# An LSTM layer on four streams: the cell's tanh, its output product and the x products take other places in their queues

## The chip, the cores and the metric

The kernel runs on one core of one Trainium2 chip. The metric is the device time of one execution in microseconds (us), lower is better. Engines are named as the profile names them: PE is TensorE (PEld its weight loads), DVE is VectorE, ACT is ScalarE, POOL is GpSimd, SP issues DMAs.

## The reference, cut to what matters

Two layers run over x of shape (128 batches, 128 nodes, 128 features), each with a residual around it. The first is a spectral layer and needs an eigendecomposition. The second, which the change touches, is two graph convolutions and then LSTM sweeps over windows of 1, 2, 3 and 4 nodes, whose last hidden state replaces the window's last node:

```python
h = relu(einsum('ts,bsh->bth', adj, h @ Wg0 + bg0))
h = relu(einsum('ts,bsh->bth', adj, h @ Wg1 + bg1))
for p in range(1, 5):
    nw = 128 // p
    wins = h[:, :nw * p, :].reshape(B * nw, p, H)
    # over the p nodes of a window, from h = c = 0:
    #   i, f, g, o = split(x_t @ Wih[p-1].T + h @ Whh[p-1].T + bias[p-1])
    #   c = sigmoid(f) * c + sigmoid(i) * tanh(g);  h = sigmoid(o) * tanh(c)
    h = h.at[:, arange(nw) * p + p - 1, :].set(last hidden state)
x = x + h
```

## The kernel before

All data is fp32. The 128 batches are done in 8 rounds (`ROUNDS`) of 16; the 16 are 4 streams (`STREAMS`, numbered 0 to 3) of 4 batches (`GB`). The first third of the time is the eigendecomposition and layer norm, then the first layer; from about 525 us the second layer runs its 8 rounds.

A round of the second layer gives each stream a linear product (LIN), a second one (ZED), a graph convolution (CONV), 11 cells, a transpose back (TURN), and the mix for the next round (TURN+1). The 11 cells (`CELLS`) are, as window size p and step j: c0 and c1 (p=1, j=0, half of the nodes each), c2 and c3 (p=2), c4 to c6 (p=3), c7 to c10 (p=4). A cell works on 256 columns for c0 to c3, on 168 for c4 to c6 and on 128 for c7 to c10. A cell with j=0 has three gates and no recurrent part; one with j>0 has four gates, each the sum of an x product (weights times the window's nodes) and a recurrent product (weights times the hidden state of the step before).

`ORDER` is a list of pairs (step n, stream i) written out by a rule, and PE, ACT and DVE each walk the same list: streams 0 and 1 do step n, then streams 2 and 3 do step n-1, and so on. So two streams' short cells (j=0) stand between the other two streams' long ones. Each engine's queue is in order; engines meet by semaphores, one set per stream, that count up once a cell:

- PE, `cell`: waits, issues the x products of gates i and f (L939), waits for `hidden_ready`, issues their recurrent products (L944), then gates g and o (L949 the x products, L952 the recurrent ones), and signals `gates_ready`. Each fp32 product appears as two matmul instructions in the trace: 16 for a cell with j>0, 6 for one with j=0. A cell with j=0 waits for `hidden_ready` of the cell before at its first product. `turn_back` (L900) also waits for it.
- ACT, `gates` (L662, one activation a gate, out of the PSUM bank) and `cell_tanh` (L670, the tanh of the cell state c). For some cells an activation of the next round's input (L635) follows.
- DVE, `cell` (i*g, f*c, their sum: L1654, L1655, L1657; only L1651 where j=0) and `hidden` (o times tanh(c): L1666, or L1668 where it writes into the node array).

In the trace, BIG holds gates i and f, PV holds g and o, spare holds cell states, tanh values and hidden states. Below, F is the activation of gate f, I, G and O those of the others, T the tanh of a cell state, and H the output product in `hidden`.

Of the kernel before, what the change touches and what calls it, by code (L numbers as in the profile page):

```python
# [33 lines left out]
GATE_I, GATE_F, GATE_G, GATE_O = range(4)  # L34
# [6 lines left out]
CELLS = [(1, 0, 0, N // 2), (1, 0, N // 2, N // 2)] + [(p, j, 0, N // p) for p in range(2, SKIPS + 1) for j in range(p)]  # L41
# [18 lines left out]
def build(nc, t_in, out):  # L60
    with ExitStack() as ctx:
# [88 lines left out]
        gates_ready, acts_ready, cell_part, cell_ready = map(per_stream, ("gates", "acts", "cellp", "cell"))  # L150
        tanh_ready, hidden_ready, turned_ready, sum_ready = map(per_stream, ("tanh", "hidden", "turned", "sum"))
# [134 lines left out]
        def nodes(v):  # L286
            return v.rearrange("p (n b) -> p n b", b=GB)
# [208 lines left out]
        def _(act):  # L496
# [157 lines left out]
            def gates(it, c, i, qs):  # L654

                p, j, _, nw = CELLS[c]
                T = GB * nw
                for q in qs:
                    if q == GATE_F and j == 0:
                        continue  # L660
                    at = (p - 1) * 4 + q
                    last = nc.scalar.activation(gate_out[q][i][:, 0:T], gate(i, q, T),  # L662
                                                ACT.Tanh if q == GATE_G else ACT.Sigmoid, bias=bias[:, at:at + 1])
                if q == GATE_F:
                    last.then_inc(acts_ready[i], 1)

            def cell_tanh(it, c, i):
                T = GB * CELLS[c][3]
# [3 lines left out]
            def second_layer(it, more):  # L672
                act.wait_ge(tables, it + 1)

                nc.scalar.activation(act_scratch[:], ln[:, 2, 0:1], ACT.Sigmoid).then_inc(tables, 1)
                waiting = None
                for n, i in ORDER:
                    c = n - CELL
                    if n == LIN:
                        act.wait_ge(lin_kept[i], it + 1)  # L680
                        nc.scalar.activation(yS[i], linS[i], ACT.Relu).then_inc(y_ready[i], 1)
                    elif CELL <= n < TURN:
                        act.wait_ge(gates_ready[i], it * len(CELLS) + c + 1)
                        gates(it, c, i, (GATE_I, GATE_G, GATE_F))
                    if waiting:
                        cell_tanh(it, *waiting)
                        waiting = None
                    if CELL <= n < TURN:
                        gates(it, c, i, (GATE_O,))
                        waiting = (c, i)  # L690
                        if more and c in NORM_AT:
                            normalize(it + 1, i, NORM_AT.index(c), h1_ready)
# [13 lines left out]
        def _(pe):  # L706
# [179 lines left out]
            def mix(it, i, later):  # L886

                pe.wait_ge(h1_ready[i], it + 1)
                if later:
                    pe.wait_ge(acts_ready[i], it * len(CELLS))  # L890
                for b in range(GB):
                    last = nc.tensor.matmul(bank[i][0][:, b * N:(b + 1) * N], hs[i][:, b * D:(b + 1) * D], adjT[:],  # L892
                                            start=True, stop=True)
                last.then_inc(mix_ready[i], 1)
# [30 lines left out]
            def cell(it, c, i):  # L925

                p, j, w0, nw = CELLS[c]
                T = GB * nw
                todo = [q for q in (GATE_I, GATE_G, GATE_F, GATE_O) if j or q != GATE_F]
                xt = window(HS[i], p, j, w0, nw)  # L930
                if c == 0:
                    pe.wait_ge(H_ready[i], it + 1)
                elif j == 0:
                    pe.wait_ge(hidden_ready[i], it * len(CELLS) + c)
                else:
                    pe.wait_ge(tanh_ready[i], it * len(CELLS) + c)
                early = [q for q in todo if q in (GATE_I, GATE_F)]
                for q in early:
                    last = nc.tensor.matmul(gate(i, q, T), wT[:, 0, p - 1, q * D:(q + 1) * D], xt,  # L939
                                            start=True, stop=(j == 0))  # L940
                if j:
                    pe.wait_ge(hidden_ready[i], it * len(CELLS) + c)
                    for q in early:
                        last = nc.tensor.matmul(gate(i, q, T), wT[:, 1, p - 1, q * D:(q + 1) * D],  # L944
                                                hS[i][:, 0:T], start=False, stop=True)
                for q in todo:
                    if q in early:
                        continue
                    last = nc.tensor.matmul(gate(i, q, T), wT[:, 0, p - 1, q * D:(q + 1) * D], xt,  # L949
                                            start=True, stop=(j == 0))  # L950
                    if j:
                        last = nc.tensor.matmul(gate(i, q, T), wT[:, 1, p - 1, q * D:(q + 1) * D],  # L952
                                                hS[i][:, 0:T], start=False, stop=True)
                last.then_inc(gates_ready[i], 1)
# [24 lines left out]
        def _(dve):  # L979
# [364 lines left out]
            for f in range(2, F):  # L1344
                c = f % 2
# [300 lines left out]
            def cell(it, c, i):  # L1646
                p, j, _, nw = CELLS[c]
                T = GB * nw
                dve.wait_ge(acts_ready[i], it * len(CELLS) + c + 1)
                if j == 0:  # L1650
                    V.tensor_tensor(cS[i][:, 0:T], gI[i][:, 0:T], gG[i][:, 0:T], ALU.mult).then_inc(cell_ready[i], 1)  # L1651
                    return
                parts = it * PARTS + sum(2 for _, jj, _, _ in CELLS[:c] if jj)
                V.tensor_tensor(gI[i][:, 0:T], gI[i][:, 0:T], gG[i][:, 0:T], ALU.mult).then_inc(cell_part[i], 1)  # L1654
                V.tensor_tensor(gF[i][:, 0:T], gF[i][:, 0:T], cS[i][:, 0:T], ALU.mult).then_inc(cell_part[i], 1)  # L1655
                dve.wait_ge(cell_part[i], parts + 2)
                V.tensor_tensor(cS[i][:, 0:T], gI[i][:, 0:T], gF[i][:, 0:T], ALU.add).then_inc(cell_ready[i], 1)  # L1657

            def hidden(it, c, i):
                p, j, w0, nw = CELLS[c]  # L1660
                T = GB * nw

                dve.wait_ge(tanh_ready[i], it * len(CELLS) + c + 1)

                if j < p - 1:
                    V.tensor_tensor(hS[i][:, 0:T], gO[i][:, 0:T], tS[i][:, 0:T], ALU.mult).then_inc(hidden_ready[i], 1)  # L1666
                else:
                    V.tensor_tensor(window(HS[i], p, j, w0, nw), nodes(gO[i][:, 0:T]), nodes(tS[i][:, 0:T]),  # L1668
                                    ALU.mult).then_inc(hidden_ready[i], 1)
# [23 lines left out]
            def second_layer(it, more, extra=None):  # L1693

                waiting = None
                for n, i in ORDER:
                    if n == LIN:
                        dve.wait_ge(lin_ready[i], it + 1)
                        V.tensor_tensor(batches(linS[i]), batches(bank[i][2]),
                                        G0[:].unsqueeze(1).to_broadcast([N, GB, N]), ALU.add).then_inc(lin_kept[i], 1)  # L1700
                    elif n == ZED:
                        dve.wait_ge(z_ready[i], it + 1)
                        V.tensor_tensor(batches(zS[i]), batches(bank[i][3]),
                                        bg1B[:].unsqueeze(1).to_broadcast([N, GB, D]), ALU.add).then_inc(z_kept[i], 1)
                    elif n == CONV:
                        dve.wait_ge(conv_ready[i], it + 1)
                        V.tensor_scalar(nodes(HS[i]).rearrange("p n b -> p b n"), batches(bank[i][0]), 0.0, None,
                                        ALU.max).then_inc(H_ready[i], 1)
                    elif CELL <= n < TURN:
                        cell(it, n - CELL, i)  # L1710
                    elif n == TURN:
                        residual(it, i)
                    elif n > TURN and more:
                        keep_mix(it + 1, i)
                    if waiting:
                        hidden(it, *waiting)
                        waiting = None
                    if CELL <= n < TURN:
                        waiting = (n - CELL, i)
                    if extra:  # L1720
                        extra(n, i)
# [30 lines left out]
```

## Time and profile before

| | us |
|---|---|
| median of 3 runs (lowest, highest) | 1285.96 (1285.43, 1286.99) |
| the profiled execution: its own time | 1288.18 |
| span of its instructions | 1286.4 |
| busy: PE | 1206.5 (94%) |
| busy: PEld | 1074.1 (83%) |
| busy: DVE | 929.1 (72%) |
| busy: ACT | 903.5 (70%) |
| busy: POOL | 338.0 (26%) |

The profiled execution lies 2.2 us over the median. Its span is 1.8 us shorter than its own time. Matmuls are pipelined: a matmul's duration in the trace is longer than the distance to the next one, so PE's busy time covers short gaps between starts.

### The profile page before, as it was taken

The numbers are of one execution on the slowest core, as the hardware profiler recorded it, in microseconds if no ns is written. First come the engines' busy times: TensorE is split into PE (matmuls) and PEld (weight loads), VectorE is DVE, ScalarE is ACT, GpSimd is POOL, SyncE is SP. The second block draws the span as 40 slices with busy tenths as digits, with TensorE's granted clock in tenths as the row PEclk, the third lists the DMA queues.
The fourth block names the chain that finished last, engine by engine and source line by source line (L and its number), as shares of the span: only waits on it lengthen the run. The fifth ranks groups of instructions, "written<-read, shape, count | busy, mean of one in ns | idle before, by whom it ended". The sixth has DMA issues, their size and how long they took to land.

```text
span 1286.4 us, 26031 instructions
## 1 busy us (share of the span) xinstructions
PE 1206.5 (94%) x7973; PEld 1074.1 (83%) x7973; DVE 929.1 (72%) x4498; ACT 903.5 (70%) x3309; POOL 338.0 (26%) x1175
## 2 busy tenths in 40 slices
PE   9999999996645799999999999999999999999997
PEld 7788888875534688889889899899899899899897
DVE  8999999999999677667745645645645655656555
ACT  6788888868972122679578578578578578587676
POOL 0488888888888300001200000000000000000000
PEclk9999999988987799999999999999999999999999
DMA  9600000000000033000100100100000000000001
GB/s 264 148 2 2 2 2 2 2 1 1 2 1 1 16 97 86 2 1 2 33 0 0 33 0 0 33 0 9 24 0 16 16 0 16 16 0 17 17 1 34
DMA packets 43629, 28.83 MB, mean 22 GB/s; under 512 B 1521, under 2 KB 39441, under 8 KB 43537
## 3 DMA queue, kind: packets, MB, share of 16 engines
q1 hardware_dynamic: 43536, 27.81, 7.9%
q8 instruction: 33, 0.54, 0.2%
q14 instruction: 60, 0.48, 0.1%
HBM read 19.42 MB, written 8.39 MB: 22 GB/s over the span
## 4 chain that ended last, share of the span: by engine, by line
PE 60%; POOL 26%; DVE 6%; issue 5%; ACT 2%; ACTq 0%; DVEq 0%; POOLq 0%
PE bank L949 15%; PE bank L939 11%; PE bank L944 9%; PE bank L952 8%; POOL leaf L477 3%; PE bank L869 2%; PE bank L921 2%; PE bank L913 2%; PE bank L877 2%; PE bank L907 2%; PE bank L884 2%; PE bank L892 2%; POOL leaf L453 2%; POOL leaf L459 2%; ACT BIG L662 1%
## 5 line engine op out<-in xcount | busy, mean ns | idle before, releaser
L662 ACT ACTIVATE BIG<-bank,bias 128x128 f32<-128x128 f32 (+2 forms) x544 | 227.3, 418 | 160.8 <-PE bank L952 101.5
L949 PE MATMUL bank<-spare,wT 128*128 128x256 f32 (+2 forms) x1408 | 311.3, 321 | 0.0
L662 ACT ACTIVATE PV<-bank,bias 128x256 f32<-128x256 f32 (+2 forms) x704 | 302.6, 432 | 0.0
L949 PEld LDWEIGHTS bank<-spare,wT 128*128 128x128 f32 x1408 | 234.8, 191 | 13.2
L939 PE MATMUL bank<-spare,wT 128*128 128x128 f32 (+2 forms) x1088 | 226.4, 319 | 4.1 <-DVE spare L1668 2.7
L1654 DVE TENSOR_TENSOR BIG<-BIG,PV 128x128 f32<-128x128 f32 (+2 forms) x192 | 63.0, 328 | 207.3 <-ACT BIG L662 207.3
L939 PEld LDWEIGHTS bank<-spare,wT 128*128 128x128 f32 x1088 | 169.5, 191 | 19.3 <-DVE spare L1668 6.1
L952 PE MATMUL bank<-spare,wT 128*128 128x128 f32 (+2 forms) x768 | 169.7, 303 | 0.0
L944 PE MATMUL bank<-spare,wT 128*128 128x128 f32 (+2 forms) x768 | 141.7, 307 | 3.7 <-DVE spare L1666 1.2
L670 ACT ACTIVATE spare<-spare 128x256 f32<-128x256 f32 (+2 forms) x352 | 133.3, 379 | 4.2 <-DVE spare L1657 3.9
L952 PEld LDWEIGHTS bank<-spare,wT 128*128 128x128 f32 x768 | 125.2, 191 | 3.3
L944 PEld LDWEIGHTS bank<-spare,wT 128*128 128x128 f32 x768 | 113.8, 191 | 14.2 <-DVE spare L1666 10.8
L1651 DVE TENSOR_TENSOR spare<-BIG,PV 128x256 f32<-128x256 f32 (+2 forms) x160 | 60.8, 380 | 86.6 <-ACT PV L662 86.5
L736 PE MATMUL bank<-base 128*128 128x256 f32 x252 | 85.5, 421 | 0.0
L643 ACT ACTIVATE PV<-bank,b 128x512 f32<-128x512 f32 x32 | 22.0, 687 | 87.2 <-PE bank L869 87.2
L1657 DVE TENSOR_TENSOR spare<-BIG 128x128 f32<-128x128 f32 (+2 forms) x192 | 62.9, 327 | 6.6
L738 PEld LDWEIGHTS bank<-A,base 128*128 128x128 f32 x254 | 37.8, 187 | 34.7 <-DVE A L1100 34.4
L635 ACT ACTIVATE ahead<-X,ln 128x128 f32 (+1 forms) x128 | 62.9, 502 | 0.0
L1655 DVE TENSOR_TENSOR BIG<-BIG,spare 128x128 f32<-128x128 f32 (+2 forms) x192 | 61.6, 321 | 0.0
L1666 DVE TENSOR_TENSOR spare<-PV,spare 128x128 f32<-128x128 f32 (+2 forms) x192 | 61.6, 321 | 0.0
L809 PE MATMUL bank<-base,ahead 128*128 128x128 f32 x128 | 23.6, 313 | 38.7 <-ACT ahead L604 21.6
L1668 DVE TENSOR_TENSOR spare<-PV,spare 128x256 f32<-128x256 f32 (+2 forms) x160 | 59.6, 373 | 0.2 <-ACT spare L670 0.2
(495 smaller groups left out, 2773.2 us busy)
## 6 DMA issues: line engine op xcount, KB each, us to landing
spare<-in_x SPq DMA_DIRECT2D x32, 256.0 KB, 3.8
out<-X SPq DMA_DIRECT2D x32, 256.0 KB, 2.4
spare<-in_L_gnn_Wih SPq DMA_DIRECT2D x4, 256.0 KB, 4.9
spare<-in_L_gnn_Whh SPq DMA_DIRECT2D x4, 256.0 KB, 4.2
W<-in_L_gnn_W SPq DMA_DIRECT2D x2, 64.0 KB, 3.2
Wg<-in_L_gnn_Wg SPq DMA_DIRECT2D x2, 64.0 KB, 2.7
adj<-in_adj SPq DMA_DIRECT2D x1, 64.0 KB, 1.8
X<-in_x SPq DMA_DIRECT2D x4, 0.5 KB, 17.7
```

Of the source, the lines that this page charges most:

```text
L635: ins = nc.scalar.activation(hs[i][:, b * D:(b + 1) * D], X[:, at, :].rearrange("p b d -> p (b d)"), ACT.Relu, bias=ln[:, 3, at], scale=ln ...
L662: last = nc.scalar.activation(gate_out[q][i][:, 0:T], gate(i, q, T), ACT.Tanh if q == GATE_G else ACT.Sigmoid, bias=bias[:, at:at + 1])
L670: nc.scalar.activation(tS[i][:, 0:T], cS[i][:, 0:T], ACT.Tanh).then_inc(tanh_ready[i], 1)
L736: nc.tensor.matmul(banks[0][:, 0:2 * N], x_wide, base[:, 0:2 * N], start=True, stop=True).then_inc(xb_ready, 1)
L939: last = nc.tensor.matmul(gate(i, q, T), wT[:, 0, p - 1, q * D:(q + 1) * D], xt, start=True, stop=(j == 0))
L944: last = nc.tensor.matmul(gate(i, q, T), wT[:, 1, p - 1, q * D:(q + 1) * D], hS[i][:, 0:T], start=False, stop=True)
L949: last = nc.tensor.matmul(gate(i, q, T), wT[:, 0, p - 1, q * D:(q + 1) * D], xt, start=True, stop=(j == 0))
L952: last = nc.tensor.matmul(gate(i, q, T), wT[:, 1, p - 1, q * D:(q + 1) * D], hS[i][:, 0:T], start=False, stop=True)
L1654: V.tensor_tensor(gI[i][:, 0:T], gI[i][:, 0:T], gG[i][:, 0:T], ALU.mult).then_inc(cell_part[i], 1)
L1655: V.tensor_tensor(gF[i][:, 0:T], gF[i][:, 0:T], cS[i][:, 0:T], ALU.mult).then_inc(cell_part[i], 1)
L1657: V.tensor_tensor(cS[i][:, 0:T], gI[i][:, 0:T], gF[i][:, 0:T], ALU.add).then_inc(cell_ready[i], 1)
L1666: V.tensor_tensor(hS[i][:, 0:T], gO[i][:, 0:T], tS[i][:, 0:T], ALU.mult).then_inc(hidden_ready[i], 1)
```

## The change

On ACT the tanh of the cell before moves from behind gates i, g and f of a cell to behind gate i alone. On DVE the output product of the cell before moves from behind the products of a cell to ahead of them. On PE the x products of a cell with j>0 no longer wait for the tanh of the stream's cell before (`tanh_ready`) but for the read of its last gate, o; for that `acts_ready` now counts twice a cell.

```diff
@@ ACT, gates
-                if q == GATE_F:
-                    last.then_inc(acts_ready[i], 1)
+                    if q in (GATE_F if j else GATE_G, GATE_O):
+                        last.then_inc(acts_ready[i], 1)
@@ ACT, second_layer
-                        gates(it, c, i, (GATE_I, GATE_G, GATE_F))
+                        gates(it, c, i, (GATE_I,))
                     if waiting:
                         cell_tanh(it, *waiting)
                         waiting = None
                     if CELL <= n < TURN:
-                        gates(it, c, i, (GATE_O,))
+                        gates(it, c, i, (GATE_G, GATE_F, GATE_O))
@@ PE, mix and cell
-                    pe.wait_ge(acts_ready[i], it * len(CELLS))
+                    pe.wait_ge(acts_ready[i], it * (2 * len(CELLS)))
...
-                    pe.wait_ge(tanh_ready[i], it * len(CELLS) + c)
+                    pe.wait_ge(acts_ready[i], it * (2 * len(CELLS)) + 2 * c)
@@ DVE, cell and second_layer
-                dve.wait_ge(acts_ready[i], it * len(CELLS) + c + 1)
+                dve.wait_ge(acts_ready[i], it * (2 * len(CELLS)) + (2 * c + 1))
...
                 for n, i in ORDER:
+                    if waiting:
+                        hidden(it, *waiting)
+                        waiting = None
                     if n == LIN:
...
-                    if waiting:
-                        hidden(it, *waiting)
-                        waiting = None
```

ACT's queue at c8 of stream 0, in the loop over the rounds; BIG is gate i and, the second time, f, PV is g and o, spare is the tanh (here of c6 of stream 3). Before:

```order
L662 ACTIVATE BIG<-bank,bias 128x128
L662 ACTIVATE PV<-bank,bias 128x128
L662 ACTIVATE BIG<-bank,bias 128x128
L670 ACTIVATE spare<-spare 128x168
L662 ACTIVATE PV<-bank,bias 128x128
L635 ISA x2
L635 ACTIVATE ahead<-X,ln 128x128
```

The same place in the changed kernel:

```order
L662 ACTIVATE BIG<-bank,bias 128x128
L670 ACTIVATE spare<-spare 128x168
L662 ACTIVATE PV<-bank,bias 128x128
L662 ACTIVATE BIG<-bank,bias 128x128
L662 ACTIVATE PV<-bank,bias 128x128
L635 ISA x2
L635 ACTIVATE ahead<-X,ln 128x128
```

The tanh stands two activations earlier, and gates g and f one later; o and what follows keep their place.

DVE's queue at c9 of stream 3 (first three products), followed by the two TURN steps (L1677, the residual sum, of streams 0 and 1). Before:

```order
L1654 TENSOR_TENSOR BIG<-BIG,PV 128x128
L1655 TENSOR_TENSOR BIG<-BIG,spare 128x128
L1657 TENSOR_TENSOR spare<-BIG 128x128
L1666 TENSOR_TENSOR spare<-PV,spare 128x128
L1677 TENSOR_TENSOR X<-X,bank 128x512
L1666 TENSOR_TENSOR spare<-PV,spare 128x128
L1677 TENSOR_TENSOR X<-X,bank 128x512
```

In the changed kernel, with the output product of c9 of stream 2 now ahead of the three and that of stream 3 behind them:

```order
L1666 TENSOR_TENSOR spare<-PV,spare 128x128
L1654 TENSOR_TENSOR BIG<-BIG,PV 128x128
L1655 TENSOR_TENSOR BIG<-BIG,spare 128x128
L1657 TENSOR_TENSOR spare<-BIG 128x128
L1666 TENSOR_TENSOR spare<-PV,spare 128x128
L1677 TENSOR_TENSOR X<-X,bank 128x512 x2
```

Every output product moves one step of the list forward, past whatever DVE does there: a cell's products, a residual sum, or the ReLU behind CONV.

PE's queue at c5 of stream 0, with the semaphores waited for (the difference, - before, + changed):

```order
 L936 REGISTER_ALU
-L939 MATMUL bank<-spare,wT 128x168 [waits tanh0]
+L939 MATMUL bank<-spare,wT 128x168 [waits acts0]
 L939 MATMUL bank<-spare,wT 128x168
+L942 REGISTER_ALU
 L944 MATMUL bank<-spare,wT 128x168 [waits hidden0]
 L944 MATMUL bank<-spare,wT 128x168
```

No matmul moves; the first wait names another semaphore, and since the two waits now need different numbers, one register instruction stands between them.

## Rows read from the trace of the kernel before

**Rows 1.** Windows: busy us by engine in one round (x is the count)
```profile
697.50:791.95 94.45, 93.51 (x626) 86.23 (x625) 54.42 (x157) 70.08 (x223) 0.00 (x0) 1.00 0.04 11
```
**Rows 2.** Waits of PEld, 525 us to the end: total us, times, longest
```profile
PEld bank L944 <- DVE spare L1666: 10.8, 32, 0.4
PEld bank L939 <- DVE spare L1668: 6.1, 9, 0.7
PEld bank L939 <- ACT spare L670: 4.2, 16, 0.4
```
**Rows 3.** Timeline of PE at a round's front: start, us, instructions, [idle before]
```profile
716.64 3.60 PE L907 MATMUL bank<-BIG,Wg 128*128 128x512 f32 x8
720.07 1.95 PE L913 MATMUL bank<-Wg,PV 128*128 128x128 f32 x16
721.91 2.05 PE L921 MATMUL bank<-adjT,spare 128*128 128x128 f32 x16
723.80 1.95 PE L913 MATMUL bank<-Wg,PV 128*128 128x128 f32 x16
725.59 0.60 PE L939 MATMUL bank<-spare,wT 128*128 128x256 f32 x2
```
**Rows 4.** Timeline of PE, starts of two neighbouring cells, 256 and 168 columns
```profile
740.53 1.03 PE L939 MATMUL bank<-spare,wT 128*128 128x256 f32 x4
...
743.98 1.03 PE L939 MATMUL bank<-spare,wT 128*128 128x256 f32 x4
...
770.32 0.73 PE L939 MATMUL bank<-spare,wT 128*128 128x168 f32 x4
...
772.60 0.73 PE L939 MATMUL bank<-spare,wT 128*128 128x168 f32 x4
```
**Rows 5.** Timeline of PE, TURN to c10 of stream 2; one round later
```profile
706.68 1.16 PE L900 MATMUL bank<-base,spare 128*128 128x128 f32 x8
708.02 0.71 PE L939 MATMUL bank<-spare,wT 128*128 128x128 f32 x4 [0.18 <-ACT spare L670]
708.88 0.71 PE L944 MATMUL bank<-spare,wT 128*128 128x128 f32 x4
709.43 0.39 PE L949 MATMUL bank<-spare,wT 128*128 128x128 f32 x2
...
802.49 0.60 PE L939 MATMUL bank<-spare,wT 128*128 128x128 f32 x3 [0.18 <-ACT spare L670]
```
**Rows 6.** Timeline of PE, last x products of c2 of stream 3
```profile
749.16 1.03 PE L949 MATMUL bank<-spare,wT 128*128 128x256 f32 x4
```
**Rows 7.** Timeline of ACT and DVE, 256 columns, around c3 of stream 1
```profile
747.64 0.47 ACT L662 ACTIVATE BIG<-bank,bias 128x256 f32<-128x256 f32 x1 [1.58 <-PE bank L952]
...
748.37 0.48 ACT L662 ACTIVATE BIG<-bank,bias 128x256 f32<-128x256 f32 x1
748.72 0.42 ACT L670 ACTIVATE spare<-spare 128x256 f32<-128x256 f32 x1
749.03 0.48 ACT L662 ACTIVATE PV<-bank,bias 128x256 f32<-128x256 f32 x1
...
750.13 0.42 ACT L670 ACTIVATE spare<-spare 128x256 f32<-128x256 f32 x1
...
750.68 0.42 DVE L1668 TENSOR_TENSOR spare<-PV,spare 128x256 f32<-128x256 f32 x1
```
**Rows 8.** Timeline of ACT and DVE, 128 columns, c10 of stream 1
```profile
703.31 0.37 ACT L662 ACTIVATE BIG<-bank,bias 128x128 f32<-128x128 f32 x1 [0.45 <-PE bank L952]
...
703.83 0.37 ACT L662 ACTIVATE BIG<-bank,bias 128x128 f32<-128x128 f32 x1
704.08 0.32 ACT L670 ACTIVATE spare<-spare 128x128 f32<-128x128 f32 x1
704.28 0.38 ACT L662 ACTIVATE PV<-bank,bias 128x128 f32<-128x128 f32 x1
...
704.76 0.29 DVE L1657 TENSOR_TENSOR spare<-BIG 128x128 f32<-128x128 f32 x1
```

## The prediction

> **What bounds the kernel now.** I read the windows first, cut to one round of the second layer. PE is busy for 93.51 of 94.45 us, ACT for 70.08 and DVE for 54.42, at the full clock (1.00) [rows 1]. So PE sets the time there, and the change, which takes no matmul away, can gain only what PE loses to waits. How much that is, busy time does not tell, because matmuls overlap; the starts do. I take the distance between starts where nothing waits: 3.43/8 = 0.429 us for 512 columns and 1.79/16 = 0.112 for 128 [rows 3], 3.45/16 = 0.2156 for 256 and 2.28/16 = 0.1425 for 168 [rows 4]. From the code a round has 8 instructions of 512 columns (LIN), 136 of 256 (per stream 6 for each of c0 to c2, 16 for c3), 152 of 168 (6+16+16) and 328 of 128 (6+16+16+16 for the cells, 28 for ZED, CONV, mix and TURN). That makes 3.4 + 29.3 + 21.7 + 36.7 = 91.1 us. The round takes 802.49 - 708.02 = 94.47 [rows 5]. PE loses some 3.3 us a round.
>
> Then I asked for the waits of the weight loads, which name who is late: 32 waits for an output product before a recurrent product (4 a round), 16 for a tanh before x products (2 a round), 9 for an output product before a short cell (1 a round) [rows 2]. The change moves just these three. One further loss, 0.15 a round, it doesn't touch: CONV of stream 0 comes 0.05 late (721.91 - 720.07 = 1.84 for 1.79) and pays another 0.10 (723.80 - 721.91 = 1.89), the weight load that a stall leaves exposed [rows 3].
>
> The Trainium skill (Perfetto Trace Analysis, Identifying the Most-Contended Engine) says that matmul busy time doesn't tell the headroom and that the weight loads' does. By matmul idle time the gain would end at (94.45 - 93.51) x 8 = 7.5 us; by the starts at 3.3 x 8 = 26 [rows 1, 3 to 5]. The starts are what I go by.
>
> **The tanh, two activations earlier; F one tanh later.** In the 128-column cells F starts 0.52 and T 0.77 after I [rows 8]. In the new order T starts 0.26 after I, if its cell state is there. Its output product H then waits for nothing else: it ends at I + 0.26 + 0.32 (T) + 0.29 (a product's length, [rows 8]) + some 0.1 for the handoffs between engines (an estimate: F to T in [rows 7] is 1.76, three products in a row and F leave about 0.1 of it) = I + 1.0. Before, H stood behind the other stream's products, which end at 705.05, 1.74 after I [rows 8], and so ended at about I + 1.95. H comes some 0.95 us earlier: about half by each of the two moves, and neither alone brings it, since T behind the products of DVE, or H ahead of them with the late T, is still late.
>
> Is that enough? The waits come where two short cells stand between. Take c9 behind c8, with c7 of streams 2 and 3 between. PE's next start is 0.2 ahead of I (749.16 - 8 x 0.216 = 747.43 against 747.64 [rows 6, 7]). It has 12 x 0.112 = 1.34 of short cells and 0.45 of its own x products to do, and needs H's data a load (0.10) earlier: I - 0.2 + 1.79 - 0.1 = I + 1.5. H at I + 1.0 is in time by 0.5; before it was late by 0.45. With 168-column short or long cells the cover is longer and the answer the same, and c1 behind c0, late by about 0.2, has T 0.36 earlier ([rows 7], half of I to F). So I cost these at nothing left.
>
> Two places keep a wait.
> - **c4 behind c3** (no x products to cover it). New order from I at 747.64: T of stream 0's c3 at +0.37, G 0.31 later, F 0.36 later, at 748.68. F to the tanh of the same cell takes 750.13 - 748.37 = 1.76 (F, three products, handoffs); so T of stream 1 at 750.44, H from 750.89 to 751.31, and with handoff and load 751.46 [rows 7]. PE's slot for c4 of stream 0 is 749.16 + 4 x 0.216 = 750.02, now met, and for stream 1 it is 6 x 0.1425 later, 750.88. The stall moves one cell on, and is 0.58 us.
> - **c10 behind c9 of stream 2**, with only the TURN steps between. This place has both waits now: 2.75 us from 706.68 to 709.43 for 16 matmuls of 1.79, so 0.9 lost, 0.41 of it at the recurrent product (0.86 for four starts of 0.45) [rows 5]. The x products go free. For H, ACT must be on time: T waits for F + 1.22 + a handoff, F to T being 1.26 (between 1.22 and 1.30), while O and the next I fill only 0.5 of it [rows 8]. After the short cells, where ACT has more to do than PE, it is late, and the loop T, G (0.20 later), F (0.25 later), T again takes 0.20 + 0.25 + 1.26 = 1.71 against PE's 16 x 0.112 = 1.79, so it catches up by only 0.08 a cell. What stays lies between 0 (ACT on time) and 0.45 (as late as now); in a run of eight such items most of the lateness survives, and I take 0.35.
>
> **The x products** wait for O of a cell whose gates were read at least two items ago; they cover 0.45 us of H's way in the sum above. **The register instruction** on PE (L942, 6 a round): the like one, L936, stands ahead of the cell at 740.53, with no gap in the sequence in which I read the distance. I take 0, and 0.1 each, one exposed load [rows 3], as the other end: 4.8 us in all.
>
> **DVE's order.** H now goes ahead of CONV's ReLU, the residual sum and the mix copy, and these wait behind a tanh and a product, 0.42 each [rows 7]. PE has two cells c1 queued ahead of the first user of that ReLU, 12 x 0.216 = 2.6 us, and for the mix copy of stream 0 three more mixes of 8 x 0.112 and the two TURN steps. Hidden; without the cover it would be some 0.8 us a place.
>
> **The sum.** Per round 3.3 - 0.15 - 0.58 - 0.35 = 2.2 us, and 8 rounds 17.8. The last round has no L635 activations, so ACT is not late at c10 (0.35 more); its very last chain has T in front of G and F, 0.20 longer [rows 8], and nothing behind to hide it. Net 17.9 us. Against the profiled execution's 1288.18 that is 1270.3; that execution stands 2.2 over the median, and from 1285.96 I get **1268.1 us**.
>
> **The rivals.**
> - *ACT becomes the bound (slower).* If the loop T, G, F, T takes more than PE's 1.79 us, every 128-column cell with j>0 pays: 12 a round. It decides from where 12 x (loop - 1.79) is over 2.2, a loop of 1.97, 0.26 over my 1.71. At 2.1 us it would cost 3.7 a round and give 1285.96 + 8 x 1.5 = 1298. For it: T now waits at the head of ACT's queue with G, F and O behind it. Against: each link has its row [rows 8], and the 256-column loop has yet more room (0.31 + 0.36 + 1.76 = 2.4 against 3.45 [rows 4, 7]).
>  The Trainium skill (ScalarE: Activation LUTs, What ACT_TABLE_LOAD costs) lets activations that follow one another overlap by about 93 ns. By that, T to G would be 0.23 and G to F 0.29, an estimate that makes the loop 1.78, at PE's pace, and what stays at c10 the whole 0.45: 0.8 us less gain in all. The trace has 0.20 and 0.25.
> - *Half the gain.* ACT's lateness also reaches c9 and c6 behind the short cells, where my cover is 0.5 us: two more waits of 0.3 to 0.5 for streams 0 and 2. Gain 1.2 a round: 1276.
> - *No change.* Each stall only moves one cell on, as at c4. Against: the others have x products and short cells as cover. 1286.
> - *All but the fixed loss goes*: (3.3 - 0.15) x 8 = 25, 1261. It needs c4's chain to be 0.58 shorter; against: every link of it stands in a row.
>
> **How the numbers follow.** A measurement of this kernel tells about 0.2% (2.6 us) from no change. Chances: the forecast (1264 to 1272) 0.70, half the gain (to 1279) 0.14, nearly all lost waits gone (about 1261) 0.08, no change 0.03, slower 0.05. So faster 0.92, same 0.03, slower 0.05. The range that leaves out the last two and the farther halves of the second and third is 1262 to 1276; the register instructions' 4.8 us lie within it.
>
> **What the changed profile would show.** Rounds of 92.3 us. No waits of L939 for L670; L944's for L1666 down from 4 a round to 1, at c10 of stream 2, about 0.3; L939's for L1668 still 1 a round, now at c4 of stream 1. T 0.26 behind I where ACT is on time, and new short idle stretches of ACT ahead of L670, released by L1657. It would be wrong if ACT's loop exceeded 1.79 us, if the lateness of ACT reached c6 and c9, or if a gap stood ahead of every L944 (the register instruction).

## The result

| | before | changed |
|---|---|---|
| median (lowest to highest, 4 runs each) | 1286.37 (1285.43 to 1286.99) | 1266.48 (1265.86 to 1266.71) |
| ratio, 95% interval | | 0.9847 (0.9835 to 0.9859) |
| span of the profiled execution | 1286.4 | 1265.0 |
| a round of the second layer | 94.46 | 91.95 |

The change makes the kernel 19.9 us faster, and the interval of the ratio lies clear of 1. 17.9 were forecast, and 1266.48 lies in the range.

One round of the changed kernel in the windows view (columns as in [rows 1]):

```profile
690.30:782.25 91.95, 91.63 (x627) 85.87 (x626) 57.03 (x157) 70.68 (x223) 0.00 (x0) 1.00 0.04 12
```

The same matmuls in 2.5 us less. ACT and DVE run as many instructions as before (223 and 157). DVE shows 2.6 us more busy time for them: the durations of neighbours in its queue overlap less than they did, and each instruction is about as long as before. The waits of the weight loads over the second layer, to be compared with [rows 2], show which waits went:

```profile
PEld bank L939 <- DVE spare L1668: 4.8, 8, 0.8
PEld bank L913 <- ACT PV L681: 3.8, 7, 1.4
PEld bank L900 <- DVE spare L1668: 2.9, 4, 1.2
PEld bank L944 <- DVE spare L1666: 0.7, 1, 0.7
```

The 16 waits for a tanh (L670) are gone, and of the 32 for an output product ahead of a recurrent one (L944) a single one is left, in the first round. The wait of L939 for L1668 stays, once a round. The waits of L913 for ACT's ReLU (L681) at a round's front are loads that come early: in the middle rounds the matmuls of L913 lose no time by their starts, and only the one of 1.4 us, ahead of the second round, costs PE something (see e9). Those of L900 lie at the end of the first round and in the last one. The timeline of PE shows where the wait of L939 is now, at c4 of stream 1 (it was at stream 0):

```profile
743.38 0.45 PE L939 MATMUL bank<-spare,wT 128*128 128x168 f32 x2
743.66 0.73 PE L949 MATMUL bank<-spare,wT 128*128 128x168 f32 x4
744.72 0.55 PE L939 MATMUL bank<-spare,wT 128*128 128x168 f32 x2 [0.32 <-DVE spare L1668]
745.10 0.59 PE L949 MATMUL bank<-spare,wT 128*128 128x168 f32 x3
```

From 743.66 to 745.10 are 1.44 us for six starts of 0.1425, 0.86: the stall costs 0.58. ACT and DVE at the same place, to be compared with [rows 7]:

```profile
740.99 0.47 ACT L662 ACTIVATE BIG<-bank,bias 128x256 f32<-128x256 f32 x1 [1.58 <-PE bank L952]
741.36 0.41 ACT L670 ACTIVATE spare<-spare 128x256 f32<-128x256 f32 x1
741.67 0.47 ACT L662 ACTIVATE PV<-bank,bias 128x256 f32<-128x256 f32 x1
742.02 0.47 ACT L662 ACTIVATE BIG<-bank,bias 128x256 f32<-128x256 f32 x1
...
743.78 0.42 ACT L670 ACTIVATE spare<-spare 128x256 f32<-128x256 f32 x1 [0.56 <-DVE spare L1657]
...
744.23 0.43 DVE L1668 TENSOR_TENSOR spare<-PV,spare 128x256 f32<-128x256 f32 x1 [0.48 <-ACT spare L670]
```

The order is I, the tanh of stream 0, G, then F at 742.02, 1.03 behind I. From F to the tanh of the same cell it is 1.76; then H follows. The tanh now makes ACT wait 0.56 us, which costs nothing except through H.

### The profile page after: what moved, and what is told of

Read it like the earlier page. It is cut to its first block, busy times and chain, and to the rows that moved or that the text cites. A ratio compares the mean times of both kernels' runs of the same rounds, so it can differ in the third digit from the quotient of the medians.

```text
span 1265.0 us, 26139 instructions
## 1 busy us (share of the span) xinstructions
PE 1191.1 (94%) x7973; PEld 1070.5 (85%) x7973; DVE 949.4 (75%) x4498; ACT 908.5 (72%) x3309; POOL 335.2 (27%) x1175
## 4 chain that ended last, share of the span: by engine, by line
PE 48%; POOL 26%; issue 18%; DVE 4%; ACT 1%; POOLq 1%; DMA 1%; SPq 0%; DVEq 0%
PE bank L949 14%; PE bank L939 11%; PE bank L952 7%; PE bank L944 7%; POOL leaf L477 3%; PE bank L921 2%; POOL leaf L453 2%; PE bank L913 2%; POOL leaf L459 2%; PE bank L892 2%; PE bank L907 2%; POOL leaf L474 1%; POOL leaf L414 1%; POOL leaf L421 1%; PE bank L900 1%
## 5 line engine op out<-in xcount | busy, mean ns | idle before, releaser
L949 PE MATMUL bank<-spare,wT 128*128 128x256 f32 (+2 forms) x1408 | 311.3, 321 | 0.0
L662 ACT ACTIVATE PV<-bank,bias 128x256 f32<-128x256 f32 (+2 forms) x704 | 278.0, 425 | 0.0
L949 PEld LDWEIGHTS bank<-spare,wT 128*128 128x128 f32 x1408 | 234.8, 191 | 13.2
L939 PE MATMUL bank<-spare,wT 128*128 128x128 f32 (+2 forms) x1088 | 223.0, 315 | 2.7 <-DVE spare L1668 2.7
L939 PEld LDWEIGHTS bank<-spare,wT 128*128 128x128 f32 x1088 | 170.5, 191 | 12.6 <-DVE spare L1668 4.8
L952 PE MATMUL bank<-spare,wT 128*128 128x128 f32 (+2 forms) x768 | 169.7, 303 | 0.0
L670 ACT ACTIVATE spare<-spare 128x256 f32<-128x256 f32 (+2 forms) x352 | 129.3, 367 | 21.8 <-DVE spare L1657 17.3
L1668 DVE TENSOR_TENSOR spare<-PV,spare 128x256 f32<-128x256 f32 (+2 forms) x160 | 60.7, 380 | 107.5 <-ACT spare L670 107.5
L944 PE MATMUL bank<-spare,wT 128*128 128x128 f32 (+2 forms) x768 | 138.5, 303 | 0.5 <-DVE spare L1666 0.5
L944 PEld LDWEIGHTS bank<-spare,wT 128*128 128x128 f32 x768 | 114.4, 191 | 4.0 <-DVE spare L1666 0.7
L1657 DVE TENSOR_TENSOR spare<-BIG 128x128 f32<-128x128 f32 (+2 forms) x192 | 63.0, 328 | 6.6
```

What stands on the lines that cost most here:

```text
L670: nc.scalar.activation(tS[i][:, 0:T], cS[i][:, 0:T], ACT.Tanh).then_inc(tanh_ready[i], 1)
```

## The experiments

"Round" is the distance between the starts of LIN on PE (L907 or its line in that kernel) in two neighbouring rounds near the middle of the second layer. From the third round to the seventh it repeats within 0.01 us in a trace, except for one round of `e5_wide_tanh`, which is 1.5 us longer than its neighbours (see there). So it tells more than the time does. The rows it is taken from, one pair shown, of the changed kernel:

```profile
894.07 0.59 PE L907 MATMUL bank<-BIG,Wg 128*128 128x512 f32 x1
...
986.02 0.59 PE L907 MATMUL bank<-BIG,Wg 128*128 128x512 f32 x1
```

| kernel | round | median | ratio to before (95%) |
|---|---|---|---|
| before | 94.46 | see below | 1 |
| changed | 91.95 | 1266.48 | 0.9847 (0.9835, 0.9859) |
| e1_tanh | 96.50 | 1305.32 | 1.0137 (1.012, 1.0153) |
| e2_out | 93.40 | 1278.98 | 0.993 (0.9913, 0.9946) |
| e3_x | 94.46 | 1288.04 | 1.0003 (0.9994, 1.0013) |
| e4_tanh_out | 92.14 | 1270.26 | 0.9866 (0.9849, 0.9882) |
| e5_wide_tanh | 95.03 | 1294.2 | 1.0064 (1.0049, 1.008) |
| e6_early_ig | 91.61 | 1262.68 | 0.9817 (0.9803, 0.983) |
| e7_early_var | 91.94 | 1266.87 | 0.9848 (0.9833, 0.9863) |
| e8_both | 91.60 | 1262.2 | 0.9814 (0.98, 0.9827) |
| e9_short_inverse | 91.94 | 1264.56, one run | |
| e10_tanh_behind_g | 92.21 | 1268.18, one run | |

Each ratio is to runs of the kernel before on the same chip in the same series. Its median was 1286.37 beside the changed kernel, 1287.63 beside e1 to e4 and 1286.68 beside e5 to e8, so the ratios compare better than the medians. For e9 and e10 there is one run each, beside one of the kernel before (1285.7), and their rounds carry the argument.

### One part alone

**e1_tanh**, only ACT's order (the signal for the gates read still counts once a cell):

```diff
-                if q == GATE_F:
-                    last.then_inc(acts_ready[i], 1)
+                    if q == (GATE_F if j else GATE_G):
+                        last.then_inc(acts_ready[i], 1)
...
-                        gates(it, c, i, (GATE_I, GATE_G, GATE_F))
+                        gates(it, c, i, (GATE_I,))
...
-                        gates(it, c, i, (GATE_O,))
+                        gates(it, c, i, (GATE_G, GATE_F, GATE_O))
```

> The kernel before with the tanh moved behind the first gate on ACT, and nothing else. Theory A (the gain comes from the two moves together; the output product H is what PE waits for): H still stands behind the next cell's products on DVE, and these now start one tanh later (0.20 to 0.31 us), so H and the next tanh come later at every place where short cells stand between. Slower: a round of 96.4 us instead of 94.46, 1285.96 + 8 x 1.9 = 1301. Theory B (each move brings its share alone): about half of the gain, a round of 93.2, 1276. Theory C (the x products' wait is the cause): the tanh is released earlier, so the 2 waits a round for it go, a round of 93.6, 1279.

Measured: the round grows by 2.04 us. Its waits over one round, from the waits view:

```profile
PEld bank L944 <- DVE spare L1666: 2.6, 4, 0.9
PEld bank L939 <- DVE spare L1668: 2.2, 5, 1.0
```

No wait for a tanh is left. The waits for H grew: those of L944 are 2.6 us against 1.4 in a round before. L939 waits for its H five times where it waited once; among these are c4, now for two streams, c1 and c7. DVE and ACT at a 128-column cell show why:

```profile
889.11 0.37 ACT L662 ACTIVATE BIG<-bank,bias 128x128 f32<-128x128 f32 x1
889.37 0.30 ACT L670 ACTIVATE spare<-spare 128x128 f32<-128x128 f32 x1
...
890.22 0.29 DVE L1654 TENSOR_TENSOR BIG<-BIG,PV 128x128 f32<-128x128 f32 x1 [0.92 <-ACT BIG L662]
...
890.95 0.29 DVE L1666 TENSOR_TENSOR spare<-PV,spare 128x128 f32<-128x128 f32 x1
```

The tanh starts 0.26 behind I, but H ends at 891.24, 2.13 behind I, where the prediction read 1.95 in the kernel before. This is theory A: the tanh is early, but H stands behind products that start later. B and C fall.

**e2_out**, only DVE's order:

```diff
                 for n, i in ORDER:
+                    if waiting:
+                        hidden(it, *waiting)
+                        waiting = None
...
-                    if waiting:
-                        hidden(it, *waiting)
-                        waiting = None
```

> The kernel before with the output product ahead of the next cell's products on DVE, and nothing else. Theory A: H then waits for the late tanh only, which comes 0.77 us behind the first gate; H is some 0.5 us earlier where it was late by 0.45, the waits for the tanh ahead of x products stay. A round of 93.3, 1286 - 9 = 1277. Theory B (additive, half each): 93.2, 1276. Theory C (the x wait): unchanged, 94.5, 1286.

Measured: 1.06 us a round less. Over one round:

```profile
PEld bank L939 <- DVE spare L1668: 0.9, 1, 0.9
PEld bank L939 <- ACT spare L670: 0.6, 2, 0.4
```

The four waits of L944 are gone, those for the tanh stay. By the round's length A and B can't be told apart here (93.3 and 93.2); e1 excludes B.

**e3_x**, only the counter, which counts twice a cell as in the change, and PE's wait:

```diff
...
-                    pe.wait_ge(tanh_ready[i], it * len(CELLS) + c)
+                    pe.wait_ge(acts_ready[i], it * (2 * len(CELLS)) + 2 * c)
```

> The kernel before with the x products waiting for the last gate's read instead of the tanh (with the counter that counts twice), and nothing else. Theory A: the x products start earlier, but the recurrent products behind them wait for the same H as before, so PE loses the same time a few matmuls later. No change: a round of 94.3 to 94.5, 1286. Theory C: the 2 waits a round for the tanh go, 0.7 to 0.9 us a round, 1279.

Measured: no change. The timeline of PE at c10 of stream 2, to be compared with [rows 5]:

```profile
705.21 1.15 PE L900 MATMUL bank<-base,spare 128*128 128x128 f32 x8
706.20 0.61 PE L939 MATMUL bank<-spare,wT 128*128 128x128 f32 x4
707.40 0.71 PE L944 MATMUL bank<-spare,wT 128*128 128x128 f32 x4 [0.59 <-DVE spare L1666]
707.95 0.39 PE L949 MATMUL bank<-spare,wT 128*128 128x128 f32 x2
```

From L900 to L949 it is 2.74 us, as in [rows 5] (2.75). The x products start with no wait, and the recurrent ones wait longer. C falls: the two waits for a tanh in [rows 2] cost nothing of their own.

**e4_tanh_out**, both moves, PE waiting for the tanh as before; shown against the changed kernel, and the counter counts once a cell again:

```diff
...
-                    pe.wait_ge(acts_ready[i], it * (2 * len(CELLS)) + 2 * c)
+                    pe.wait_ge(tanh_ready[i], it * len(CELLS) + c)
```

> The changed kernel with the x products waiting for the tanh again, as before: both moves, no new wait on PE. Theory A: nearly the whole gain, a round of 92.0 against 91.95 for the full change, up to 0.2 more at c10 of stream 2, where only the transposes stand between; 1267 to 1268. Theory C: most of the gain is lost, a round of 92.8 or more, 1274.

Measured: 92.14, 0.19 a round over the full change. The x wait is worth 8 x 0.19 = 1.5 us once the tanh and H are early, and nothing alone. H's move together with the x wait, without the tanh's move, was not run, so what the tanh's move adds to those two is not known apart.

### The position, and ACT's loop

**e10_tanh_behind_g**:

```diff
-                        gates(it, c, i, (GATE_I,))
+                        gates(it, c, i, (GATE_I, GATE_G))
...
-                        gates(it, c, i, (GATE_G, GATE_F, GATE_O))
+                        gates(it, c, i, (GATE_F, GATE_O))
```

> The changed kernel with the tanh behind gates i and g instead of behind i alone. Theory A (what counts is when H is there, and there is a margin at most places): H comes one activation later (0.25 to 0.36 us) where ACT is on time, F comes no earlier or later. Only c1 of stream 0 (0.16) and c10 of stream 2 (0.16) lose their margin: a round of 92.2 against 91.94, 1268 to 1268.5. Theory J (being at the first place is what gives the gain): the round goes back towards 93.4, the value with the tanh at its old place, 1273 or more.

Measured: 92.21. The first place is worth 0.27 us a round over the second; J falls.

**e5_wide_tanh** lengthens the suspected loop:

```diff
                 act.wait_ge(cell_ready[i], it * len(CELLS) + c + 1)
+                T = 384 if T == 128 else T
                 nc.scalar.activation(tS[i][:, 0:T], cS[i][:, 0:T], ACT.Tanh).then_inc(tanh_ready[i], 1)
```

> The changed kernel, in which the tanh of the 128-column cells runs over 384 columns (the extra 256 are not used, so the outputs stay the reference's): ACT's loop tanh, G, F, tanh grows from 1.71 to 1.92 us, above PE's 1.79 a cell. Theory A (the rival priced in the prediction: ACT becomes the bound from 1.79 on, at 12 cells a round): 12 x 0.13 = 1.6 us a round more, less what was in time by a margin, so 93.3 to 93.5 a round and 1266.5 + 11 to 13 = 1278 to 1280; the new waits of PE stand at c9, c10 and the transposes. Theory D (the loop has slack elsewhere, since ACT is busy for only three quarters of the time): under 0.4 us a round, 1267 to 1270.

Measured: 95.03, so 3.1 us a round more, where A said 1.4 to 1.6 and D under 0.4. ACT's timeline in this kernel:

```profile
886.63 0.52 ACT L671 ACTIVATE spare<-spare 128x384 f32<-128x384 f32 x1
887.06 0.35 ACT L662 ACTIVATE PV<-bank,bias 128x128 f32<-128x128 f32 x1
887.31 0.36 ACT L662 ACTIVATE BIG<-bank,bias 128x128 f32<-128x128 f32 x1
...
888.56 0.52 ACT L671 ACTIVATE spare<-spare 128x384 f32<-128x384 f32 x1
```

The tanhs stand 1.93 apart, against PE's 1.79, and PE waits at the transposes, here those of another round:

```profile
800.38 0.64 PE L901 MATMUL bank<-base,spare 128*128 128x128 f32 x4
802.12 0.75 PE L901 MATMUL bank<-base,spare 128*128 128x128 f32 x4 [1.10 <-DVE spare L1669]
```

So the mechanism of the slower rival exists: a loop of 1.71 costs nothing in the middle rounds, one of 1.93 does. Its price of 12 x (loop - 1.79) is too low by half. PE doesn't lose the time cell by cell. By the starts of a middle round, 1.4 of the 3.1 us stand at the transposes, where the wait is 1.10, 1.0 at c10 of stream 2 right behind them, and the rest at the 128-column cells around and at the next round's front; nothing is lost at c7. ACT's lateness adds up over the cells and PE pays it where nothing covers. What the price leaves out is, I think, the four short cells c7: there PE needs 6 x 0.112 = 0.67 and ACT is the longer one anyway, so 0.21 more for each tanh counts in full (0.8), and H itself ends 0.21 later at each of the two places that wait. 1.7 + 0.8 + 0.4 = 2.9. That is argued, not shown apart.

The one round that is 1.5 us longer has its cause in the windows view, where the column behind POOL's is the granted clock as a share of the full one:

```profile
1089.30:1092.80 3.50, 3.50 (x18) 3.50 (x19) 2.27 (x6) 1.85 (x6) 0.00 (x0) 0.53 0.01 4
```

Here the granted clock is 0.53, the lower level (1.2 GHz) but for the edges; in the rest of the round it is 1.00 (2.4 GHz). The 128-column matmuls in this stretch start 0.213 apart instead of 0.112, which makes the 1.5 us. PE had stood idle for 1.09 and 0.73 us in the 3.2 us before. The other middle rounds of this kernel have the same two stalls and keep the clock; the first round also has such a stretch. So the stalls alone don't decide it. No run shows what does. The changed kernel shows no such stretch in the second layer before its last round's end.

### What is still left

**e6_early_ig**:

```diff
+                    elif j and q == GATE_G:
+                        last.then_inc(relu_ready[i], 1)
...
-                dve.wait_ge(acts_ready[i], it * (2 * len(CELLS)) + (2 * c + 1))
...
+                dve.wait_ge(relu_ready[i], ROUNDS + it * (PARTS // 2) + sum(1 for _, jj, _, _ in CELLS[:c] if jj) + 1)
                 V.tensor_tensor(gI[i][:, 0:T], gI[i][:, 0:T], gG[i][:, 0:T], ALU.mult).then_inc(cell_part[i], 1)
+                dve.wait_ge(acts_ready[i], it * (2 * len(CELLS)) + (2 * c + 1))
```

> The changed kernel, in which DVE's product i times g waits for gate g alone, not for f, in cells with j>0. Theory A (the wait left at c4 of stream 1 is the chain F, three products, tanh, H): F to tanh is shorter by one product's start distance, 0.34 us at 256 columns, so the wait there falls from 0.58 to 0.24. A round of 91.6, 1264 (0.2% below the changed kernel). Theory E (the wait at c4 is set elsewhere, by ACT's order or DVE's queue): no change, 91.95, 1266.5.

Measured: 91.61, 0.34 less. DVE and ACT at c3 of stream 1 in this kernel, where i times g is L1657 and the tanh L672:

```profile
740.16 0.47 ACT L662 ACTIVATE BIG<-bank,bias 128x256 f32<-128x256 f32 x1
...
740.30 0.43 DVE L1657 TENSOR_TENSOR BIG<-BIG,PV 128x256 f32<-128x256 f32 x1
740.67 0.42 DVE L1659 TENSOR_TENSOR BIG<-BIG,spare 128x256 f32<-128x256 f32 x1
...
741.59 0.42 ACT L672 ACTIVATE spare<-spare 128x256 f32<-128x256 f32 x1 [0.22 <-DVE spare L1661]
```

i times g now runs beside F, and F to the tanh is 741.59 - 740.16 = 1.43 instead of 1.76. E falls; the wait left at c4 is this chain. The time fell by more than the 2.7 us expected, to 1262.68: the middle rounds bring 0.34 each, but the first brings 1.13 (92.53 us against 93.66) and the last with what follows it 0.8. In the first round the wait at c10 of stream 2 (the row at 609.09 below) is gone in this kernel, so that wait too hangs on the chain from F to the tanh.

The first two rounds of the changed kernel take 93.66 and 92.85, not 91.95. Three kernels ask why.

**e7_early_var** and **e8_both** (this edit and the last):

```diff
-                elif (n, i) == (CELL + 8, 3):
+                elif (n, i) == (CELL + 7, 3):
```

> The changed kernel, in which the six variance instructions of the first round stand four items of the list earlier, so that POOL's power of 10.58 us starts about 4.9 us earlier. Theory F (the first two rounds gained less, 2.2 and 1.9 us against 2.5, because POOL's power ends late and holds DVE's inverse, the mix copies and so the front of the second round): the front of the second round loses 0.7 us less and the first round's c10 wait of 0.68 goes; rounds 1 and 2 together 1.2 to 1.7 us shorter, 1265. Theory G (it is the batch statistics on DVE alone, not POOL): no change, 1266.5.

> The changed kernel with both of the last two edits (i times g early, variance early). If A and F hold, they add: 0.34 x 8 + 1.5 = 4.2 us, 1262.3.

Measured for e7: POOL's power of 10.58 us now runs from 597.62 instead of 603.98 and so ends at 608.20, the first round shrinks by 0.36 to 93.30, and the second stays at 92.85. Of PE's three idle stretches there in the changed kernel,

```profile
609.09 0.71 PE L944 MATMUL bank<-spare,wT 128*128 128x128 f32 x4 [0.51 <-DVE spare L1666]
616.74 0.74 PE L900 MATMUL bank<-base,spare 128*128 128x128 f32 x4 [0.21 <-DVE spare L1668]
621.59 0.38 PE L913 MATMUL bank<-Wg,PV 128*128 128x128 f32 x1 [0.55 <-ACT PV L681]
```

the first stays in e7,

```profile
609.57 0.71 PE L944 MATMUL bank<-spare,wT 128*128 128x128 f32 x4 [0.51 <-DVE spare L1666]
```

and so does that of L913, by its starts as long as before (0.71). Only that of the transposes (L900) is gone. Theory F is right for 0.36 us and wrong for the rest: it expected the c10 wait and the front to shrink too. Its median, 1266.87, can't be told from the changed kernel's.

e8 reaches 1262.2 where 1262.3 was expected, and part of that is luck. By the rounds the early product i times g brings 4.0 us instead of 2.7, and the early variance 0.8 on top of it instead of 1.5: the first round is 91.81, 0.72 less than in e6. The medians of e6 and e8 are within each other's intervals.

**e9_short_inverse**:

```diff
-                    inverse(slice(FIRST, BATCH))
+                    V.reciprocal(ln[:, 3, FIRST:BATCH], ln[:, 2, FIRST:BATCH]).then_inc(ln_done, 1)
```

> The changed kernel, in which the inverse of the first round is one instruction of DVE instead of six, so that the norm scales of the last 64 batches are wrong: it leaves out about 1.2 us of DVE's work at the end of the first round. The variance moved earlier left the 0.71 us wait at the second round's front as it was, so POOL is not its cause. Theory H (DVE comes to the mix copies and to the sums behind LIN late because of the six instructions): the wait of ZED's products for ACT at the second round's front falls from 0.71 to 0.15 or less, the second round from 92.85 to 92.1, and the transposes' wait of 0.38 at the end of the first goes. Theory I (it is something else in the unrolled first round, as the longer walk of code): the second round stays at 92.85.

This kernel leaves out five of the six instructions, so its outputs are not the reference's. Measured: the second round takes 92.02, the first 93.14. PE at the second round's front:

```profile
616.61 3.17 PE L907 MATMUL bank<-BIG,Wg 128*128 128x512 f32 x7
619.61 2.03 PE L913 MATMUL bank<-Wg,PV 128*128 128x128 f32 x16
```

Without the five instructions there is no 0.7 us wait ahead of L913. Theory H holds, I falls: DVE's own queue carries the inverse at the moment when the faster PE comes to the next round's front. The transposes' wait at the end of the first round goes here as it went in e7, so the two edits don't add up there. Of the 2.6 us that the first two rounds take over two middle ones, e9 removes 1.35. The rest, 1.3 us, is nearly all in the first round, 0.8 of it at c10 of stream 2; whether DVE's batch statistics cause it (theory G) no run separates.

## Why the prediction was right

- **What bounds.** PE's losses to waits, 3.3 us a round by the starts of its matmuls, were the right measure. 2.52 of it went. That is more in one round than the 0.94 us in which PE shows no busy matmul, and eight rounds gave far more than the 7.5 us that this would allow.
- **c4** keeps a stall of 0.58, one cell later, as worked out. e6 shows that it is the chain from F to the tanh.
- **c10 of stream 2: the one term that was mis-sized.** 0.35 was taken; in the middle rounds it is 0. The tanhs of ACT in that stretch:

```profile
694.88 0.31 ACT L670 ACTIVATE spare<-spare 128x128 f32<-128x128 f32 x1
...
696.59 0.31 ACT L670 ACTIVATE spare<-spare 128x128 f32<-128x128 f32 x1
...
698.30 0.31 ACT L670 ACTIVATE spare<-spare 128x128 f32<-128x128 f32 x1 [0.18 <-DVE spare L1657]
...
700.01 0.31 ACT L670 ACTIVATE spare<-spare 128x128 f32<-128x128 f32 x1
...
701.72 0.31 ACT L670 ACTIVATE spare<-spare 128x128 f32<-128x128 f32 x1
702.06 0.29 DVE L1666 TENSOR_TENSOR spare<-PV,spare 128x128 f32<-128x128 f32 x1 [0.37 <-ACT spare L670]
...
702.09 0.61 PE L939 MATMUL bank<-spare,wT 128*128 128x128 f32 x4
...
702.43 0.53 PEld L944 LDWEIGHTS bank<-spare,wT 128*128 128x128 f32 x4
...
702.54 0.61 PE L944 MATMUL bank<-spare,wT 128*128 128x128 f32 x4
```

 The loop is 1.71 us, the forecast value, and catches up 0.08 a cell. Over the four intervals that is 0.3, most of the lateness instead of little of it, and H, done at 702.35, is in time for a weight load at 702.43, by less than 0.1 us. The prediction's own terms said so: eight items at 0.08 make 0.64, more than the 0.45 that it started from, so "most of the lateness survives" did not follow from them. In the first round the same place does stall (the 609.09 row above), for 0.8 by the starts.
- **The x wait** brings nothing alone (e3) and 0.19 a round in company (e4). The prediction used it as a cover for H's way, and that is what it is.
- **"Neither alone brings it"** was half right. The tanh's move alone costs 2.04 us a round; H's move alone brings 1.06, 42% of the whole. The gain was not "about half by each": H's place is the part that pays by itself, and the tanh's pays only with it.
- **The ends.** The second layer's last round with what follows it took 97.5 us before and 95.1 now: 2.4 less, against 2.35 in the sum. The first two rounds gained 2.17 and 1.94, less than the middle ones. The variance, the inverse and the stall at c10 of the first round (e7, e9, e6) are not in the prediction.
- **The sum.** Rounds: 2.17 + 1.94 + 5 x 2.52 + 2.4 = 19.1 us. Forecast 17.9: the 0.35 at c10, in seven rounds, is 2.5 too little. Against that the first two rounds gained 1.0 less than the sum then gives, and the five middle ones 0.05 less each. So errors of opposite sign met, and the forecast is nearer than its terms. The rest of the 19.9 is within what executions differ by ahead of the second layer: LIN of the first round starts between 523.0 and 526.0 us in these traces, in kernels that don't differ there.
- **The rivals.** ACT's loop as the bound is real but not reached (e5). The register instruction costs nothing: in the rows above L944 starts 0.45 behind L939, four starts of 0.112, and e3, which has it, takes the same round as before.

The lowest median here is that of the changed kernel with i times g early and the variance early (e8), 0.9814 (0.98 to 0.9827) of before; e6 can't be told from it.

## What to carry to other kernels

Count what a saturated engine loses by the distances between starts, not by its idle time, and then follow, for each wait, the whole path of the value that is late: a wait at its end (here H, the output product) can hide behind an earlier wait (here the tanh), and removing the earlier one alone can even cost time, as here. Where a value passes two in-order queues, moving it forward in one may cost in the other; try the moves together and apart. After a gain, look at once-only work in the unrolled first round: part of it was hidden by the slack that has just been removed.

## What was not expected of the hardware

A stalled PE pays for more than the wait: after each stall listed here the next matmul starts about 0.10 us later than its distance, in the rows at 744.72 (0.38 for two starts of 0.1425), at 707.40 in e3 (0.55 for four of 0.112) and in [rows 3]. I read this as the weight load that the stall leaves exposed; no run changes the load to show it. The 0.10 doesn't grow with the wait, so short waits are dear: CONV of stream 0 in [rows 3] comes 0.05 late and loses 0.15.
